# The attention pass of a graph network: two drains carry TensorE's signals, values move ahead of the lift, results leave a chunk later

## The reference, cut to what matters

```python
def _L2_gnn_ref(feat, W_src, b_src, W_dst, b_dst, W_v, b_v, src, dst):
    f_src = feat @ W_src.T + b_src
    f_dst = feat @ W_dst.T + b_dst
    f_v = feat @ W_v.T + b_v
    a = f_src[src] + f_dst[dst]            # one row an edge
    e = where(a >= 0, a, 0.2 * a)
    sa = edge_softmax(e, dst)              # over the edges of one destination, per feature
    rst = segment_sum(f_v[src] * sa, dst)
    return rst
...
h = jnp.maximum(_layernorm(x), 0.0)
x = x + _L2_gnn_ref(h, ..., src, dst)
```

## Time and profile before

| | us |
|---|---|
| median of three runs | 2885.24 (2883.45 to 2888.44) |
| span of the profiled execution | 3922.1 |
| of it, up to the end of the large fills (0 to 415) | 415 |
| of it, scattered writes (415 to 1170) | 755 |
| of it, first two layers (1170 to 2236) | 1066 |
| of it, attention pass (2236 to 3722) | 1486 |
| of it, last layer (3722 to 3922) | 200 |

### The profile page before, as it was taken

One profiled execution on the slowest core, in us unless ns is written; L12 is line 12 of the kernel. 1 busy time (PEld: TensorE's weight loads), 2 busy tenths in 40 slices (PEclk: granted clock), 3 DMA queues, 4 the chain that ended last, 5 costly groups with the idle time before them and its releaser, 6 DMA issues.

```text
span 3922.1 us, 37110 instructions
## 1 busy us (share of the span) xinstructions
PE 2203.3 (56%) x11497; PEld 1368.2 (35%) x11497; DVE 1745.8 (45%) x2706; ACT 981.7 (25%) x1791; POOL 1607.2 (41%) x1664
## 2 busy tenths in 40 slices
PE   3111111111113666678989677777777777777389
PEld 2000000000001132454544455555555555555245
DVE  6121112111126223343423367666666666766742
ACT  0000000000001322200110145555555555555311
POOL 2766666666670000002000455555555555555300
PEclk7555555555555778878999788888888888888689
DMA  9999200000003978763358577777887777777443
GB/s 389 368 333 366 90 1 2 1 1 2 1 6 137 403 297 325 266 190 96 109 188 259 163 209 215 215 218 212 221 225 211 211 218 213 217 213 217 130 134 113
DMA packets 509104, 724.18 MB, mean 185 GB/s; under 512 B 70756, under 2 KB 366621, under 8 KB 509008
## 3 DMA queue, kind: packets, MB, share of 16 engines
q1 hardware_dynamic: 437444, 608.72, 47.2%
q0 software_dynamic: 65680, 109.05, 10.9%
q10 hardware_dynamic: 5884, 5.21, 0.4%
HBM read 402.27 MB, written 320.51 MB: 184 GB/s over the span
## 4 chain that ended last, share of the span: by engine, by line
PE 36%; another core or an unknown queue 28%; DVE 12%; issue 9%; DMA 8%; ACT 7%; SPq 0%; ACTq 0%; POOL 0%; DVEq 0%; POOLq 0%
PE PS L677 8%; DMA G<-adj_d 7%; PE PS L981 5%; PE PS L951 4%; PE PS L960 4%; PE PS L976 3%; PE PS L1006 2%; DVE V L1648 2%; PE PS L811 2%; PE PS L975 1%; DVE V L1649 1%; ACT OSF L1266 1%; ACT M L1259 1%; ACT D L1277 1%
## 5 line engine op out<-in xcount | busy, mean ns | idle before, releaser
L595 POOL DMA_INDIRECT G<-tab_sv,src_e x784 | 768.3, 980 | 648.7 <-PE PS L677 395.5
L605 POOL DMA_INDIRECT adj_d<-D,place x782 | 752.9, 963 | 410.3 <-issue 240.7
L733 PE MATMUL PS<-G,V 128*128 128x4 bf16 x391 | 41.8, 171 | 885.3 <-issue 488.5
L981 PE MATMUL PS<-M,ident 128*128 128x512 f32 x392 | 272.7, 785 | 334.3 <-ACT M L1259 247.4
L733 PEld LDWEIGHTS PS<-G,V 128*128 128x128 bf16 x391 | 33.6, 104 | 973.0 <-issue 529.2
L1656 DVE TENSOR_REDUCE D<-PS 128x8 f32<-128x24 f32 x98 | 17.5, 178 | 714.7 <-remote 710.8
L1955 DVE TENSOR_TENSOR_SCAN RB<-mring,RB,PS 128x512 f32<-128x512 bf16 x196 | 250.3, 1277 | 139.3 <-PE PS L981 132.6
L1935 DVE TENSOR_TENSOR_SCAN HTx<-PS,HTx,D 128x512 f32<-128x512 f32 x196 | 250.9, 1280 | 90.7 <-remote 49.2
L976 PE MATMUL PS<-VT 128*128 128x128 f32 x1568 | 287.1, 285 | 0.0
L595 POOL DMA_INDIRECT wlast<-wsum_d,last_i x25 | 23.9, 957 | 627.7 <-DVE last_i L1867 620.4
L1266 ACT ACTIVATE OSF<-PS 128x512 f32<-128x512 f32 x392 | 212.3, 593 | 269.9 <-PE PS L677 160.6
(11 more groups left out here) (402 smaller groups left out, 4694.3 us busy)
## 6 DMA issues: line engine op xcount, KB each, us to landing
frac_d<-OSF SPq DMA_DIRECT2D x196, 512.0 KB
adj_d<-RB SPq DMA_DIRECT2D x7, 12800.0 KB, 44.0
G<-adj_d SPq DMA_DIRECT2D x161, 512.0 KB, 6.1
run_d<-RB SPq DMA_DIRECT2D x4, 12992.0 KB
VT<-run_d SPq DMA_DIRECT2D x196, 256.0 KB
wts_d<-X SPq DMA_DIRECT2D x149, 256.0 KB, 6.3
mring<-cut_d SPq DMA_DIRECT2D x196, 128.0 KB
HTx<-seg_d SPq DMA_DIRECT2D x196, 128.0 KB
```

Of the source, the lines that this page charges most:

```text
L595: pool.indirect_dma_start(dest, None, table, bass.IndirectOffsetOnAxis(ap=idx, axis=0)).then_inc(done, 16)
L605: pool.indirect_dma_start(adj_d, bass.IndirectOffsetOnAxis(ap=place[:, 2 * w + k:2 * w + k + 1], axis=0), pay[:, w, k, :], None).then_inc( ...
L981: nc.tensor.matmul(PS[:, q, :], ident[:, :], Ee[:, q, :], start=False, stop=True, skip_group_check=True).then_inc(leaky, 1)
```

## The change

PE no longer signals by its matmuls in this pass. Two drain instructions a chunk carry two counters instead: `fronts` after `front(c + 1)`, and `difs` after the subtraction of c, `values(c + 1)` and `lift(c + 1)`. Between these, `values` now comes before `lift`. `turn_back(c - 2)` comes after the second drain and has no signal of its own: the next step's `fronts` covers it. So ACT's `take_out` runs one chunk later, behind `fifth` and ahead of the relus, and DVE's `denominator` waits for `fronts` of the step after. All who waited for `dif`, `leaky` or `gv` wait for `difs`; SP's loads too. DVE's `heads` moves ahead of `weighted` and `denominator`. ACT's second body is unrolled as well.

```diff
@@ -307,19 +307,16 @@
         osem = sem("osem")
         zsem = sem("zsem")
         carried = sem("carried")
-        leaky = sem("leaky")
-        back = sem("back")
         ev = sem("ev")
         odma = [sem(f"odma{q}") for q in range(2)]
-        ga = sem("ga")
-        gv = sem("gv")
+        fronts = sem("fronts")
         ge = sem("ge")
         gx = sem("gx")
         gp = sem("gp")
         gfront = sem("gfront")
         gback = sem("gback")
         hm = sem("hm")
-        dif = sem("dif")
+        difs = sem("difs")
         dn0 = sem("dn0")
         segm = sem("segm")
         segst = sem("segst")
@@ -509,7 +506,7 @@
                     for h in range(R):
                         c = i * R + h
                         if not last:
-                            sp.wait_ge(dif, c + 1)
+                            sp.wait_ge(difs, c + 2)
                             load(h, c + R)
                         if not (first and h < 2):
                             store(h % 2, c - 2)
@@ -654,8 +651,7 @@
                 for c in range(NC):
                     h = c % R
                     if c >= R:
-                        pool.wait_ge(ga, c - R + 1)
-                        pool.wait_ge(gv, c - R + 1)
+                        pool.wait_ge(difs, c - R + 1)
                     for k in range(CT):
                         t = c * CT + k
                         rows_of(G[:, h, k, :], tab_sv, src_n[:, t:t + 1], ggath[h])
@@ -973,52 +969,58 @@
                     for k in range(CT):
                         o = PS[:, q, k * P:(k + 1) * P]
                         nc.tensor.matmul(o, G[:, h, k, 0:F], ident[:, :], is_transpose=True, start=k == 0, stop=False, skip_group_check=True)
-                        last = nc.tensor.matmul(o, GZ[:, h, k, :], HM[:, q, k * P:(k + 1) * P], start=False, stop=False, skip_group_check=True)
-                    last.then_inc(ga, 1)
+                        nc.tensor.matmul(o, GZ[:, h, k, :], HM[:, q, k * P:(k + 1) * P], start=False, stop=False, skip_group_check=True)
+                    pe.drain().then_inc(fronts, 1)
 
                 def lift(q, c):
                     pe.wait_ge(ge, c + 1)
-                    nc.tensor.matmul(PS[:, q, :], ident[:, :], Ee[:, q, :], start=False, stop=True, skip_group_check=True).then_inc(leaky, 1)
+                    nc.tensor.matmul(PS[:, q, :], ident[:, :], Ee[:, q, :], start=False, stop=True, skip_group_check=True)
 
                 def values(h, c, young):
 
                     q = h % 2
                     if not young:
                         pe.wait_ge(gback, GB * (c - 2) + 1)
-                    turn4(6 + q, [G[:, h, k, F:2 * F] for k in range(CT)]).then_inc(gv, 1)
+                    turn4(6 + q, [G[:, h, k, F:2 * F] for k in range(CT)])
 
                 def turn_back(q, c, young):
                     pe.wait_ge(gback, GB * c + GB)
                     if not (young and q == 0):
                         pe.wait_ge(ev, c)
                     turn4(2, [ST[:, q, k * P:(k + 1) * P] for k in range(CT)])
-                    turn4(3, [DN[:, q, k * P:(k + 1) * P] for k in range(CT)]).then_inc(back, 1)
+                    turn4(3, [DN[:, q, k * P:(k + 1) * P] for k in range(CT)])
 
                 def body(i, first, final):
                     for h in range(R):
                         c, q = i * R + h, h % 2
                         if not (final and h == R - 1):
                             front(i + (h + 1) // R, (h + 1) % R, c + 1, first and h < 1)
+                        else:
+                            pe.drain().then_inc(fronts, 1)
 
                         pe.wait_ge(gfront, GF * c + 1)
                         if q == 0:
                             pe.wait_ge(carried, i * (R // 2) + h // 2 + 1)
                         nc.tensor.matmul(PS[:, q, :], nident[:, :], RB[:, q * CE:(q + 1) * CE], start=False, stop=False, skip_group_check=True)
-                        nc.tensor.matmul(PS[:, q, :], nidentb[:, :], mring[:, h, :], start=False, stop=True, skip_group_check=True).then_inc(dif, 1)
+                        nc.tensor.matmul(PS[:, q, :], nidentb[:, :], mring[:, h, :], start=False, stop=True, skip_group_check=True)
                         if not (final and h == R - 1):
+                            values((h + 1) % R, c + 1, first and h < 1)
                             lift(1 - q, c + 1)
-                            values((h + 1) % R, c + 1, first and h < 1)
+                        pe.drain().then_inc(difs, 1)
                         if not (first and h < 2):
                             turn_back(q, c - 2, first)
                 front(0, 0, 0, True)
+                values(0, 0, True)
                 lift(0, 0)
-                values(0, 0, True)
+                pe.drain().then_inc(difs, 1)
                 body(0, True, False)
                 with nc.Fori(1, IT - 1, engines=(pe.engine,), head_slot={pe.engine: 0}) as i:
                     body(i, False, False)
                 body(IT - 1, False, True)
+                pe.drain().then_inc(fronts, 1)
                 for c in (NC - 2, NC - 1):
                     turn_back(c % 2, c, False)
+                    pe.drain().then_inc(fronts, 1)
 
             st = {"mm": 0, "gr": 0, "inv": 0, "tv": 0}
             for r in range(2):
@@ -1253,25 +1255,28 @@
             def att_pass():
                 def fifth(q, c, young):
 
-                    act.wait_ge(ga, c + 1)
+                    act.wait_ge(fronts, c + 1)
                     if not young:
-                        act.wait_ge(leaky, c - 1)
+                        act.wait_ge(difs, c - 1)
                     nc.scalar.activation(Ee[:, q, :], PS[:, q, :], ACT.Relu, scale=-0.8).then_inc(ge, 1)
 
                 def take_out(q, c, k):
-                    act.wait_ge(back, c + 1)
+                    act.wait_ge(fronts, c + 5)
                     if k is not None:
                         act.wait_ge(odma[q], 16 * k)
                     for b, o in ((2, 0), (3, F)):
                         last = nc.scalar.activation(OSF[:, q, :, o:o + F], PS[:, b, :].rearrange("p (k f) -> p k f", f=F), ACT.Copy)
                     last.then_inc(ev, 1)
 
-                def body(i, first, final):
+                def body(i, young, final):
+                    first = young and i == 0
                     for h in range(R):
                         c, q = i * R + h, h % 2
                         if not (final and h == R - 1):
                             fifth(1 - q, c + 1, first and h < 1)
-                        act.wait_ge(dif, c + 1)
+                        if not (first and h < 3):
+                            take_out(1 - q, c - 3, None if young and c < 5 else i * 2 + (h - 3) // 2)
+                        act.wait_ge(difs, c + 2)
                         if not (first and h < 2):
                             act.wait_ge(gback, GB * (c - 2) + GB)
                         nc.scalar.activation(D01[:, q, CE:2 * CE], PS[:, q, :], ACT.Relu, scale=-1.0)
@@ -1279,17 +1284,14 @@
                         act.wait_ge(gx, c + 1)
                         nc.scalar.activation(D01[:, q, CE:2 * CE], D01[:, q, CE:2 * CE], ACT.Exp, scale=-1.0)
                         nc.scalar.activation(PS[:, 4 + q, :], PS[:, 4 + q, :], ACT.Exp, scale=-1.0).then_inc(gp, 1)
-                        if first and h >= 2:
-                            take_out(q, c - 2, None)
-                        elif not first:
-                            take_out(q, c - 2, i * 2 + h // 2 - 1)
                 fifth(0, 0, True)
                 body(0, True, False)
-                with nc.Fori(1, IT - 1, engines=(act.engine,), head_slot={act.engine: 0}) as i:
+                body(1, True, False)
+                with nc.Fori(2, IT - 1, engines=(act.engine,), head_slot={act.engine: 0}) as i:
                     body(i, False, False)
                 body(IT - 1, False, True)
-                for c in (NC - 2, NC - 1):
-                    take_out(c % 2, c, NC // 2 - 1)
+                for c in (NC - 3, NC - 2, NC - 1):
+                    take_out(c % 2, c, c // 2)
 
             for t in range(2):
                 o = t * 13
@@ -1923,13 +1925,13 @@
 
                     q = h % 2
                     dve.wait_ge(gp, c + 1)
-                    dve.wait_ge(gv, c + 1)
+                    dve.wait_ge(difs, c + 1)
                     v.tensor_tensor(NV[:, q, :], D01[:, q, CE:2 * CE], PS[:, 6 + q, :], ALU.mult).then_inc(gback, 1)
 
                 def denominator(h, c, young, chunk0):
                     q = h % 2
                     if not young:
-                        dve.wait_ge(back, c - 1)
+                        dve.wait_ge(fronts, c + 3)
                     if not chunk0:
                         dve.wait_ge(gback, GB * c)
                     v.tensor_tensor_scan(DN[:, q, :], PS[:, 4 + q, :], D01[:, q, CE:2 * CE], DN[:, 1 - q, CE - 1:CE], ALU.mult, ALU.add).then_inc(gback, 1)
@@ -1945,21 +1947,17 @@
```

(10 more changed lines are left out.)

## The result

The changed kernel takes **3038.8 us** (median of 4 runs, 3034.8 to 3039.7) against 2884.3 for the kernel before (4 runs, 2880.5 to 2888.4). The ratio is 1.0532, with a 95% interval of 1.0517 to 1.0547: 154 us slower. The forecast was 2963, with a range of 2845 to 3050. The sign and the range held, the range by 11 us, and half of the loss was missing.

What follows compares the result with a forecast made beforehand. The prediction took a PE-ACT loop of 5.65 us, with DMA at 5.61 to 5.95, to bound the changed kernel: (5.80 - 5.40) x 195 = 78 us on 2885.2 gives 2963 us, range 2845 to 3050.

Steps and rivals of the forecast that it cites:

- The step before, 5.40: Attention pass: the kernel before takes 5.40 us a chunk in timed runs, between DVE's 5.05 and at most 5.47.
- The step after, 5.80: Attention pass: the changed kernel takes 5.80 us a chunk, from a PE-ACT loop of 5.65 and DMA's 5.61 to 5.95.
- 0.88 of turning back: PE's turning back, 0.88 us, lies beside ACT's relus of 1.20 us and adds nothing to the loop.
- The two drains, 0.21 each: PE's two drains a chunk each add 0.21 us, from 0 to 0.38, raising the loop from 5.23 to 5.65.
- Lateness in the runs: TensorE's late signals, seen in the attention pass and scattered writes, belong to the profiled execution, 1036.9 us longer than the runs.
- The 339 us of my account: Work outside the pass needs 1738 us, 339 more than a full-length pass leaves; so the pass is at most 1147 us.
- The faster rival: PE's signals in the pass are late in runs too, a drain's increment isn't: 2838 us, down to 2612; chance 0.24.
- DMA sets both: Transfers set the pass's step, 5.5 us before and 5.6 after, hiding the longer loop: +20 us, 2905; chance 0.13.
- Loads come late: Landing over 8 us makes loads stop DVE's `heads`, then the front: 6.2 us a step, 3109 us; chance 0.05.
- DVE hidden, 1 us left: DVE's maximum waits for values too, but its 3.77 us of other work covers the 2.53 us and two hand-overs.
- ACT's `take_out`: Moved ahead of the relus, it lasts about 1.1 us and ends before values and lift; a late store stops the loop.
- the other signs: Undisturbed steps: front 0.1 us behind second relu, PE idle before, subtraction 1.5 to 1.9 behind front's start, scans 5.6 to 6.0 apart.

Runs made afterwards that it cites:

- Experiment 11: Kernel before with POOL's gathers in the pass replaced by one plain transfer a chunk from ACT's queue: 2845.0 us, ratio 0.9832, prompt chip (kernel before 2884 to 2889).
- after: The changed kernel as profiled, against the kernel before; profile span 3037.7 us, timed runs 3038.8 us, on the sort of chip where the kernel before takes 2884.3.
- Experiment 1: The kernel before, unchanged, profiled again on a late chip (kernel before 3921 to 3954 us): profile 3945.3 us, timed runs' median 3948.7 us.
- experiment 5: The changed kernel, unchanged, against the kernel before on a late chip: 3808.9 us, ratio 0.9701.
- experiment 9: Kernel before plus two bare drains a chunk on PE, without signals, in the change's places; late chip: 3958.6 us, ratio 1.0013.
- experiments 2 and 6: Changed kernel with `fronts` and `difs` signalled by matmuls instead of drains; two late chips: 3784.1 us (0.9582) and 3761.2 us (0.9601) against the kernel before.
- Experiments 3 and 4: Changed kernel, subtraction's matmul signalling again; SP's loads wait for it in the first, ACT's relus in the second: 0.9694 and 1.0170 against the kernel before, late chip.
- 7 and 8: Changed kernel, subtraction's matmul signalling again; SP's loads wait for it in the first, ACT's relus in the second: 0.9633 and 0.9744 against before, another late chip.

## Why the prediction was right or wrong

**The step before, 5.40: this term failed.** It was 5.08 (the times and the rest of 1894 us), so 0.32 x 195 = 62 of the missing 76 us are here. It lay within the bounds, 5.05 and 5.47, and I went to the upper end because of DMA, by dividing GB/s by the share in a profile from a late chip. Experiment 11 shows 324 GB/s at a share of 1.02, after shows 267 at 0.94, and the earlier trace rows itself has 363 at 0.98 in the fills: a share isn't a fraction of a fixed rate, and the quotient bounded nothing. Had I gone by the earlier trace rows alone, the sum would have been (5.80 - 5.05) x 195 = 146, or 3031.

That would have been in part luck, since DVE isn't full at 5.05. The two intervals of the earlier trace rows are 5.23 and 4.86, and the longer one has a wait for ACT in it:

```profile
2885.00 0.69 DVE L1927 TENSOR_TENSOR M<-D,PS 128x512 f32<-128x512 f32 x1 [0.21 <-ACT PS L1281]
```

Experiment 11 went under this "least", to 4.83.

**The step after, 5.80: nearly right.** It was 5.86, which is the other 12 us of (5.86 - 5.80) x 195. The place was right (relus behind values, lift and drain). The size was right in part by luck: signals cost 0.15 and 0.14 where I had none, the subtraction was 0.1 longer behind its drain, values waited 0.1 for `weighted`, the relus were 0.11 shorter, the drains cheaper than I had them. I also let DMA's 5.61 to 5.95 raise 5.65 to 5.80; nothing in the runs shows such a limit, the loop was itself 5.82. And I compared the loop with DVE and DMA only. The nearest rival was PE's own round, 4.58 in the earlier trace rows and 5.67 now, which I didn't add up with its drains: the "0.88 of turning back" beside the relus is 0.33 + 1.06.

**The two drains, 0.21 each.** The first costs 0.34 + 0.10 on the loop. The second costs PE 0.47, but beside the relus; ACT hears 0.15 us after the lift's end where it heard 0.12 after the subtraction's in the earlier trace rows, so 0.03 on the loop. The forecast's 5.23 goes from ends, so the overlap of 0.16 in the 0.34 is indeed already out of it. Counted as the forecast counts, the two are 0.18 + 0.10 + 0.03 = 0.31 against 0.42: nearly all in the first, where I had them equal.

**Lateness in the runs.** That lateness belongs to the profiled execution was wrong as a mechanism and right as a number for the runs that count. The 339 us of my account spoke against it in the timed runs, and there it was indeed absent. Experiment 1 shows why: it goes with the chip, or its state. "A faster profile is no faster run" falls: on late chips profile and runs are both faster, on the prompt chip both slower. (The 64 waits of the earlier trace rows are those of `fifth`, L1259, as the forecast says, not of the first of the two relus.) My two figures for the profile of after on such a chip, 3649 with lateness ended and 4000 without, are both off: experiment 5 has 3792.6.

**The faster rival** (0.24) named the right condition, lateness dearer than the lengthened loop, and on late chips it comes true. But its reason, that a drain's increment isn't late, falls: experiment 9 has no gain from drains, and experiments 2 and 6 gain at least as much without them.

**DMA sets both** (0.13) falls: DMA moved 310 GB/s in the step before and 267 in the step after, so its rate isn't what holds the step after. **Loads come late** (0.05): the lead is 8.28 us, as "over 8" said, but that is not ample, since `heads` waits at its end in 166 of 196 chunks. The wait is there, the consequence is small: not 6.2 us a step but some 0.1 more.

**DVE hidden, 1 us left.** So it is, by 0.8 to 0.9, but it shows in another place than I said: DVE waits ahead of `heads`, not ahead of the maximum. The scan of the maximum waited for the drain 12 times, 8.9 us in all. **ACT's `take_out`** ahead of the relu was harmless: it is over by 2401.64 in the step above, and the relu starts at 2403.01. Of the other signs two came out: the front 0.14 us behind the second relu, the subtraction 1.5 to 1.9 behind the front's start (1.60 in the step shown, 1.70 on average). Scans are 5.86 apart on average, but only 62 of 195 are within 5.6 to 6.0. "PE is idle there before" did not come out: the turning back fills that time.

## What to carry to other kernels

A signal moved behind more work lengthens every loop that runs through it. Go round that loop with the timeline, from ends to starts, with some 0.15 us for each hand-over, and compare the sum with the busiest engine's time and with the round of each engine in the loop, its drains included. Several loops can lie within 0.2 us of each other, as three do here; then mending one gives little. When a profile's span and the timed runs disagree by a third, suspect different conditions, as here: take only the undisturbed steps of that profile as the durations, take their waits out before you call an engine full, and don't extrapolate its GB/s.

## What the runs showed of the hardware

- **The same program takes 2884 to 2889 or 3921 to 3954 us, by the chip or its state**, and on one chip at one time the runs lie within some 1.3%. The loss stands in the two stages that hold POOL's indirect transfers: PE's and DVE's 98 blocks take 183 us or 1039, an attention step 5.1 (by the sum above) or 7.2 to 7.3. In the pass, increments of PE come up to 4 to 6 us after the matmul's modelled end. In the scattered writes it is more: in experiment 5 PE's matmuls of block 91 end at 1044.2, and DVE's L1658, which waits for them alone and has been idle since 1056.3, starts at 1078.3, 34 us behind them. It starts over 10 us behind in 49 of the 98 blocks; in the profile of after it is 1.27 us in nearly all. Its cause stays open. It isn't the profiler (experiment 1), and two bare drains a chunk don't change it (experiment 9). Whether it needs indirect transfers wasn't settled, since experiment 11 ran on a prompt chip.
- **A change's sign may depend on it**: 1.0532 on a prompt chip, 0.9701 on a late one, for one and the same kernel.
- **Late chips differ among themselves.** Experiments 3 and 4 put the same increment on the same matmul, on one chip: with SP waiting for it the ratio is 0.9694, with ACT's relus 1.0170. On the next chip the same two kernels (7 and 8) are at 0.9633 and 0.9744. So the relus' wait is the dearer one on both, by 5% and by 1%. I have no shown reason for that.
- **A drain between back-to-back matmuls** costs PE 0.34 us of lost overlap and drain ahead of the subtraction, and 0.10 in the subtraction behind it, and 0.47 ahead of the turning back; two a chunk were worth some 0.24 us a step on a late chip.
- **A DMA share near 1 came with quite different rates**: 267 GB/s at 0.94 in the pass of after, 324 at 1.02 in that of experiment 11, 362 at 0.99 in the fills.
